# Moving the final layer norm of a block behind the statistics of the next one, with statistics columns of its own

## The reference, cut to what matters

```
def _layernorm(x, eps=1e-5):  m = mean(x); v = var(x); return (x - m) / sqrt(v + eps)

x = x + _layernorm(attention(_layernorm(x)))   # linear attention, 16 heads of 64, then @ Wo.T + bo
x = x + _layernorm(ffn(_layernorm(x)))         # 1024 -> 4096 -> 1024, fixed-point rounding,
                                               # piecewise-linear gelu
```

## Time and profile before

| | |
|---|---|
| median of the runs | 8131.52 us (2 runs, 8122.6 and 8140.43) |
| the profiled execution | 8128.89 us |
| span of its slowest core (core 6) | 8127.4 us; the cores lie between 8082.6 and 8127.4 us |
| mean granted TensorE clock, by core | 0.727 to 0.733 of full speed |

### The profile page before, as it was taken

The page is one execution under the profiler, slowest core; times in us unless marked ns, Lnnn a source line. Parts: engine busy times, 40 slices in busy tenths (PEclk is TensorE's granted clock), DMA queues, the critical chain, the costliest instruction groups (busy, mean ns, idle before and its releaser), DMA issues.

```text
span 8127.4 us, 85997 instructions; the slowest of 8 cores (8082.6 to 8127.4 us)
## 1 busy us (share of the span) xinstructions
PE 4813.4 (59%) x24896; PEld 2670.1 (33%) x24896; DVE 3432.1 (42%) x6804; ACT 2710.4 (33%) x4129; POOL 1405.7 (17%) x1204
## 2 busy tenths in 40 slices
PE   0075556656656666666647565666665756666665
PEld 0043333333333333333324333333333433333332
DVE  1122444444532444444442244444453234444445
ACT  0032333333332333333333233333333233333333
POOL 1000222222200122222220022222220012222222
PEclk9986777777777777777778667767776766666666
DMA  5501111111121111111120111111112021111111
GB/s 174 194 27 37 52 52 55 58 57 55 55 70 40 40 57 57 53 52 52 56 80 27 37 52 52 52 58 58 55 55 73 11 65 55 52 55 55 55 55 47
DMA packets 124030, 475.62 MB, mean 59 GB/s; under 512 B 14742, under 2 KB 14999, under 8 KB 119467
## 3 DMA queue, kind: packets, MB, share of 16 engines
q1 hardware_dynamic: 100268, 369.44, 14.9%
q0 software_dynamic: 23296, 100.67, 3.6%
HBM read 419.72 MB, written 50.33 MB: 58 GB/s over the span
## 4 chain that ended last, share of the span: by engine, by line
DVE 33%; PE 24%; ACT 24%; issue 10%; DMA 5%; DVEq 2%; POOL 1%; ACTq 1%; SPq 0%; POOLq 0%
DVE poolF L946 6%; ACT poolF L230 4%; ACT poolF L941 3%; ACT poolF L936 3%; DVE poolF L950 3%; DVE poolF L954 3%; ACT poolF L958 3%; ACT poolF L962 3%; DVE poolF L217 3%; DVE poolF L823 2%; DMA poolF<-w_d 2%; DVE poolF L969 2%; PE psT L261 2%; PE psA L433 2%; PE psB L433 2%
## 5 line engine op out<-in xcount | busy, mean ns | idle before, releaser
L261 PE MATMUL psT<-idb,poolB 128*128 128x128 bf16 x1536 | 194.4, 307 | 1850.5 <-ACT poolB L793 769.7
L946 DVE TENSOR_SCALAR poolF<-poolF 128x512 f32<-128x512 f32 x512 | 527.6, 1030 | 1303.2 <-ACT poolF L941 1303.2
L965 POOL TENSOR_TENSOR poolF<-poolF 128x512 f32<-128x512 f32 x512 | 652.4, 1274 | 2448.3 <-ACT poolF L962 1878.7
L958 ACT ACTIVATE poolF<-poolF,cb 128x512 f32<-128x512 f32 x512 | 416.4, 813 | 1224.0 <-DVE poolF L954 1223.6
L261 PEld LDWEIGHTS psT<-idb,poolB 128*128 128x128 bf16 x1536 | 149.9, 139 | 1912.8 <-issue 1912.8
L973 POOL TENSOR_TENSOR poolF<-poolF 128x512 f32<-128x512 f32 x512 | 656.4, 1282 | 74.3 <-POOL poolF L965 1.3
L606 PE MATMUL psG<-lnf,wa 128*128 128x256 bf16 x2048 | 355.3, 332 | 505.1 <-ACT poolB L612 499.4
L843 PE MATMUL psA<-w2b,poolB 128*128 128x512 bf16 x1024 | 480.1, 469 | 188.1 <-DVE poolB L828 187.8
L925 PE MATMUL psF<-lnf,w1sb 128*128 128x256 bf16 x3584 | 508.5, 304 | 15.7 <-ACT poolF L941 15.7
L843 PE MATMUL psB<-w2b,poolB 128*128 128x512 bf16 x1024 | 483.8, 472 | 0.0
L843 PE MATMUL psC<-w2b,poolB 128*128 128x512 bf16 x1024 | 481.3, 470 | 0.0
(11 more groups left out here) (178 smaller groups left out, 7932.1 us busy)
## 6 DMA issues: line engine op xcount, KB each, us to landing
w2b<-wsc SPq DMA_DIRECT2D x512, 512.0 KB, 3.6
xbuf<-xin SPq DMA_DIRECT2D x48, 512.0 KB, 3.8
xbuf<-xin POOLq DMA_DIRECT2D x48, 512.0 KB, 4.9
yout<-poolF POOLq DMA_DIRECT2D x32, 512.0 KB, 3.0
yout<-poolF SPq DMA_DIRECT2D x32, 512.0 KB, 2.6
poolF<-w_d SPq DMA_DIRECT2D x16, 512.0 KB
poolF<-w_d POOLq DMA_DIRECT2D x16, 512.0 KB, 6.7
poolF<-w_d SPq DMA_DIRECT2D x8, 1024.0 KB
```

Of the source, the lines that this page charges most:

```text
L261: ttok = p.emit("T", lambda tt, src_slot=src_slot, dc=dc: tt.transpose(psT[:, dc * 128:(dc + 1) * 128], in_=poolB[:, src_slot + dc * 128:s ...
L946: xi4t = p.emit("V", lambda v, SL_A=SL_A, SL_B=SL_B: v.tensor_scalar(out=pf(SL_B, 512), in0=pf(SL_A, 512), scalar1=4.0, scalar2=4.0 * M1, ...
L958: y0t = p.emit("S", lambda s_, SL_E=SL_E, SL_D=SL_D: s_.activation(out=pf(SL_E, 512), in_=pf(SL_D, 512), func=AF.Gelu, scale=cb[:, CB_1:CB ...
L965: dtk = p.emit("G", lambda g_, SL_A=SL_A, SL_F=SL_F, SL_E=SL_E: g_.tensor_tensor(out=pf(SL_A, 512), in0=pf(SL_F, 512), in1=pf(SL_E, 512), ...
```

## The change

Three edits:

- `ln_stats` gets a parameter `base`, the first of its nine columns. The final norm (`rest`) passes `ST0B` = 7712, nine columns that nothing else uses, and all others keep `ST0`.
- `state["sq_guard"]` becomes a dictionary with one token for each base.
- The call of `fin_rest()` goes from ahead of the Wo matmuls to a place inside the loop over `s`: for s=0, behind `ln_stats` on psA and psB and ahead of n1.

```diff
+        ST0B = 7712
...
-        def ln_stats(srcs, eps_ap, scale_ap, bias_ap, wait_first=()):
+        def ln_stats(srcs, eps_ap, scale_ap, bias_ap, wait_first=(), base=None):
             wv = list(wait_first)
+            if base is None:
+                base = ST0
+
+            def st_(i):
+                return poolF[:, base + i:base + i + 1]
...
-                gw = wv + ([state["sq_guard"]] if state["sq_guard"] else [])
+                gw = wv + ([state["sq_guard"].get(base)] if state["sq_guard"].get(base) else [])
...
-            state["sq_guard"] = vtok
+            state["sq_guard"][base] = vtok
...
-                if fin_rest is not None:
-                    fin_rest()
-
                 ffn_guard = []
...
                     _, rtok = ln_stats([b0[:], b1_[:]], cb[:, CB_EPSLN:CB_EPSLN + 1], stat(S_R), stat(S_NMR),
                                        wait_first=[wo_mt[s]])
+                    if s == 0 and fin_rest is not None:
+                        fin_rest()
+                        fin_rest = None
                     n1 = p.emit("S", lambda s_, b0=b0: s_.activation(
                         out=pf(LNT, 512), in_=b0[:], func=AF.Identity,
                         scale=stat(S_R), bias=stat(S_NMR)),
...
                             _, rtok = ln_stats([xi2ap], cb[:, CB_EPS4:CB_EPS4 + 1],
-                                               stat(S_R), stat(S_NMR),
-                                               wait_first=[xt2s[s2]])
+                                               stat2(S_R), stat2(S_NMR),
+                                               wait_first=[xt2s[s2]], base=ST0B)
                             p.emit("V", lambda v, xi2ap=xi2ap: v.tensor_scalar(
-                                out=xi2ap, in0=xi2ap, scalar1=stat(S_R),
-                                scalar2=stat(S_NMR), op0=ALU.mult, op1=ALU.add),
+                                out=xi2ap, in0=xi2ap, scalar1=stat2(S_R),
+                                scalar2=stat2(S_NMR), op0=ALU.mult, op1=ALU.add),
                                 waits=[rtok])
```

More of the change, by code:

```diff
@@ L195, in stat, with stat2 @@
             return poolF[:, ST0 + i:ST0 + i + 1]
+        def stat2(i):
+            return poolF[:, ST0B + i:ST0B + i + 1]
         psA = pst_("psA", [128, 512], F32)
@@ L217, in ln_stats @@
                     rtoks.append(p.emit("V", lambda v, s=s: v.reduce_sum(
-                        out=stat(S_S1), in_=s, axis=AXX), waits=wv, inc=True))
+                        out=st_(S_S1), in_=s, axis=AXX), waits=wv, inc=True))
                 else:
                     rtoks.append(p.emit("V", lambda v, s=s: v.reduce_sum(
-                        out=stat(S_M), in_=s, axis=AXX), inc=True))
-                    p.emit("V", lambda v: v.tensor_tensor(out=stat(S_S1), in0=stat(S_S1),
-                                                          in1=stat(S_M), op=ALU.add))
+                        out=st_(S_M), in_=s, axis=AXX), inc=True))
+                    p.emit("V", lambda v: v.tensor_tensor(out=st_(S_S1), in0=st_(S_S1),
+                                                          in1=st_(S_M), op=ALU.add))
             stoks = []
             for i, s in enumerate(srcs):
-                acc = stat(S_S2A) if i == 0 else stat(S_S2B)
-                gw = wv + ([state["sq_guard"]] if state["sq_guard"] else [])
+                acc = st_(S_S2A) if i == 0 else st_(S_S2B)
+                gw = wv + ([state["sq_guard"].get(base)] if state["sq_guard"].get(base) else [])
                 gw = gw + list(state["sqs_guard"])
@@ L233, in ln_stats @@
                 if i > 0:
[L234 to L235 removed]
+                    p.emit("V", lambda v: v.tensor_tensor(out=st_(S_S2A), in0=st_(S_S2A),
+                                                          in1=st_(S_S2B), op=ALU.add),
                            waits=[stoks[-1]])
             vtok = p.emit("V", lambda v, ntot=ntot: v.tensor_scalar(
[L238 to L239 removed]
+                out=poolF[:, base + S_M:base + S_MS + 1],
+                in0=poolF[:, base + S_S1:base + S_S2A + 1],
                 scalar1=1.0 / ntot, scalar2=None,
                 op0=ALU.mult), waits=[stoks[-1]], inc=True)
[L242 to L244 removed]
+            state["sq_guard"][base] = vtok
+            p.emit("V", lambda v: v.tensor_tensor(out=st_(S_VAR), in0=st_(S_M),
+                                                  in1=st_(S_M), op=ALU.mult))
             vtok2 = p.emit("V", lambda v: v.scalar_tensor_tensor(
[L246 removed]
+                out=st_(S_VAR), in0=st_(S_VAR), scalar=-1.0, in1=st_(S_MS),
                 op0=ALU.mult, op1=ALU.add), inc=True)
             sdt = p.emit("S", lambda s_, eps_ap=eps_ap: s_.activation(
[L249 removed]
+                out=st_(S_SD), in_=st_(S_VAR), func=AF.Sqrt,
                 scale=cb[:, CB_1:CB_1 + 1], bias=eps_ap), waits=[vtok2], inc=True)
             p.emit("V", lambda v, scale_ap=scale_ap: v.reciprocal(
[L252 removed]
+                out=scale_ap, in_=st_(S_SD)), waits=[sdt])
             rtok = p.emit("V", lambda v, scale_ap=scale_ap, bias_ap=bias_ap: v.scalar_tensor_tensor(
[L254 removed]
+                out=bias_ap, in0=st_(S_M), scalar=-1.0, in1=scale_ap,
                 op0=ALU.mult, op1=ALU.mult), inc=True)
```

2 lines of the change are left out of this document (1 added, 1 removed).

## The result

The changed kernel has a median of 8257.48 us (11 runs, 8241.5 to 8335.77) against 8118.49 us of the kernel before (10 runs, 8090.96 to 8151.87). The ratio is 1.0191 with a 95% interval of 1.0157 to 1.0225, some 155 us more. It compares the means of the fast runs (one of the 11 was slow, with a lower clock on one of the chip's two dies); the medians alone are 139 us apart.

The account below looks back on a forecast made before the run. The kernel was taken as bound by a relay between engines, with DVE's list the path at block boundaries. 28 boundaries x 6.68 = 187 us on the profiled 8128.9 gave 8316 us, range 8240 to 8364.

Parts of the forecast that it names:

- The order on both lists, and the swap: DVE and ACT at the boundary: fin_rest stays ahead of L781; 8.65 us wait exposed, 1.97 us of n1 and n2 hidden.
- what would show each step: Timeline signs: DVE idle 7.5 to 11 us before L217 in all 32 boundaries, table load moved, blocks near 201 us.
- L781 at 28.37 from zero: Start of the x2b addition after the last L739 ends: 8.65 + 5.98 + 13.74 = 28.37 us instead of 21.69.
- The wait of 8.65: DVE idle before the statistics on psA until PE finishes psB, 8.65 us on average, previously covered by fin_rest.
- 6.68 us per boundary: Boundary between two blocks: L781 at 28.37 instead of 21.69, 6.68 us longer, 28 times, 187 us in sum.
- The rest of a block hardly depends on the clock: After the boundary: blocks at clocks 0.76 and 0.67 take 194.2 and 194.5 us, so the delay stays whole.
- C: Later in the block: the delay is taken up, up to 3.6 us per block, 101 us back, 8215; chance 0.11.
- A: Wo at the boundary meets the full clock: wait 6.1, boundary 4.13 longer, kernel 116 us slower, 8245; chance 0.08.
- B: Wo at the boundary stays at half clock: wait 11.4, boundary 9.4 longer, 264 us, 8393; chance 0.08.
- D: Final norm runs entirely in DVE and ACT idle time: L781 at 16.5, 5.2 us earlier, kernel 7983 us; chance 0.03.
- Slower by over 2%, held at 0.75: Whole kernel: chance 0.75 of over 2% slower, against 0.23 within 2% and 0.02 faster by over 2%.
- PE's longer idle time costs nothing in clock, the stores and the end of a sequence nothing: PE idle before transposes grows 6.7 us, clock already 0.50; stores covered with over 20 us; sequence ends unchanged: 0.

Follow-up runs that it names:

- The doubled Wo: Wo matmuls of s=0 done twice over, in the changed kernel (ratio to the kernel before 1.033) and in the kernel before (0.9991).

## Why the prediction was right, point by point

- *The order on both lists, and the swap.* Right. DVE waits for PE, does the statistics, then the final norm, and n1 and n2 vanish beneath it. What was named for this step under "what would show each step" is in the traces: 268.8 us of waits (250 to 310 expected), 32 of them, the table load behind the statistics, L784 on the heels of L258, no idle time before L791.
- *L781 at 28.37 from zero.* 28.06 to 28.46 on four cores. The wait of 8.65, taken from 4 boundaries, was 8.40 over all 32. In 17 of the 256 boundaries of all cores the clock stays at 0.50 until psB is done, and psB ends at up to 11.4; in the others it rises before. The doubled Wo shows that the wait is in the open after the change and was covered before it.
- *6.68 us per boundary.* 0.3 too much. 28.37 was set against the 21.69 of one clean boundary; the mean of the 28 was 21.84 to 21.88, since some have a short pause of DVE. A term that is multiplied by 28 should come from all 28. Together with the wait: 28 x 0.3 = 8 us.
- *"The rest of a block hardly depends on the clock, and a delay at the boundary should go into the block's length whole."* This is the step that was too coarse. It rested on two blocks that happen to have nearly the same stretch from the last L946 to the next L999, in which PE does the attention matmuls of the next block: 28.7 us at a clock of 0.74, and 28.4 at 0.69, where the high level was 0.81. Over the 24 blocks of core 6 of the kernel before this stretch takes 26.5 to 31.5 us at clocks from 0.82 down to 0.57, and the block 190.6 to 197.1 (correlation 0.97). On seven of its cores the stretch gets shorter as its clock gets higher, with a correlation of -0.68 to -0.91, on the eighth hardly (-0.28); in the changed kernel it is -0.90 to -0.96 on all eight. On core 6 it took 29.2 us at a mean clock of 0.70 before and 28.3 at 0.77 after. In the profiles 0.8 us of a block came back, most of it there: 28 x 0.8 = 22 us. Against executions at the same mean clock it is 28 x 6.4 - 158 = 21 us, and the table above shows where; the interval of the ratios, about 28 us to either side, is wider than it.
- *Rivals.* C, as far as it went, was about an eighth of the delay (0.8 of 6.4 us), not all. A and B did not happen: Wo still begins at half clock and mostly meets the rise in its midst. D did not happen, and for the reason given: nothing passes in a list. The version that lays half s2=1 into the gaps reaches L802 at 15.5 on average, so D's price of 16.5 was about what the boundary can have; it needed the list written otherwise.
- *Slower by over 2%, held at 0.75.* Not settled: the interval of 1.0157 to 1.0225 lies on both sides of 1.02. What the runs settle is the sign, the mechanism and a size near 155 us.
- *PE's longer idle time costs nothing in clock, the stores and the end of a sequence nothing.* Nothing in the traces speaks against it.

## What to carry to other kernels

Work that stands ahead of a wait is free as long as the wait lasts: before moving it away to let a critical chain start, look at what that chain will wait for, and how long. Here both lists were in order, so the moved work was ahead of the chain's next step in either place, and only 8 us of cover was lost. Cut such work to the length of the wait, and put the rest under other waits of the same relay (0.9776), then ask of each wait in the relay whether the data need it (0.9692).

## What the runs showed of the hardware that I had not expected

- Half the matmuls can take nearly as long as all of them. Wo for s=0 with 8 of its 16 bf16 matmuls kept DVE waiting 8.0 us, with 16 of them 8.4, with 32 of them 11.5. In the first case the granted clock stays at 1.2 GHz until psB is done, in all 256 boundaries of the eight cores; with 16 (the changed kernel) it rises to 2.4 GHz before that in 239 of 256, with 32 in all.
- The mean granted clock differs between executions of the same program, 0.70 to 0.76, and with it the time: 8076 to 8172 us for the kernel before. That is more than half of the effect studied here, and two single profiles should be compared only with their clocks beside them. In the profiles with a lower mean, the granted clock is 0.81 instead of 1.00 in part of the stretches above 0.50, over some milliseconds of the span; the stretches at 0.50 fill about the same share.
- Equal mean clocks don't make equal stretches: at 0.755 and 0.754 over the execution, the end of a block had 0.725 in one order of the work and 0.759 in the other.
- A sum on DVE and a square on ACT that read the same 128x1024 float32 tile in SBUF at the same time take 1.22 and 1.06 us, as long as one behind the other.
